# A graph network with two expert stages on one core: blocks hand over their last stores, their semaphores and their first sums

## The reference

```
mean(v) = sum over edges into v of v[src] / max(degree, 1)
x = x + conv2(relu(conv1(norm(x))))     # first graph step; conv(v) = mean(v) @ Wl.T + b + v @ Wr.T
x = x + sum over the 2 chosen of 8 experts: gelu(norm(x) @ W1 + b1) @ W2 + b2
x = x + conv2(relu(conv1(norm(x))))     # second graph step, other weights
x = x + shared MLP + weighted sum over the 2 chosen of 4 small experts
```

## Time and profile before

| what | us |
|---|---|
| median of three runs | 1396.93 (1392.34 to 1399.44) |
| the profiled execution: time | 1399.89 |
| its span, first to last instruction | 1398.4 |
| PE busy in it | 1236.1 (88%) |
| DVE, ACT, POOL busy | 576.2, 400.8, 164.0 |
| borders, by the start of the next block's work | 85.1, 325.4, 828.9, 1030.3, 1247.0 |

### The profile page before, as it was taken

The page is one execution under the profiler, slowest core; times in us unless marked ns, Lnnn a source line. Parts: engine busy times, 40 slices in busy tenths (PEclk is TensorE's granted clock), DMA queues, the critical chain, the costliest instruction groups (busy, mean ns, idle before and its releaser), DMA issues. The chain is left out here.

```text
span 1398.4 us, 22052 instructions
## 1 busy us (share of the span) xinstructions
PE 1236.1 (88%) x7906; PEld 920.5 (66%) x7906; DVE 576.2 (41%) x1495; ACT 400.8 (29%) x798; POOL 164.0 (12%) x177
## 2 busy tenths in 40 slices
PE   5959999998999897299999929999989999979997
PEld 4647778775668674188888827755546677856675
DVE  7857777753436536200000026300024453256443
ACT  3444443431221000164446414300012211123322
POOL 4000000000000424234434410000000000000000
PEclk9979999999999987599999969999999999989999
DMA  6200000015642324435663532120036534125001
GB/s 194 72 22 9 17 17 8 17 42 126 172 134 80 107 72 131 138 61 112 123 137 61 98 80 94 38 82 27 27 92 175 149 121 127 56 87 169 19 19 35
DMA packets 133066, 117.03 MB, mean 84 GB/s; under 512 B 22690, under 2 KB 121379, under 8 KB 132992
## 3 DMA queue, kind: packets, MB, share of 16 engines
q1 hardware_dynamic: 100896, 74.71, 19.0%
q0 software_dynamic: 11984, 18.77, 7.0%
q10 hardware_dynamic: 20112, 22.56, 4.8%
HBM read 67.01 MB, written 48.99 MB: 83 GB/s over the span
## 5 line engine op out<-in xcount | busy, mean ns | idle before, releaser
L1242 PE MATMUL b_pa<-adj,l_parts 128*128 (+1 forms) x1100 | 144.6, 286 | 1.9 <-ACT ring L1164 1.9
L1180 ACT ACTIVATE adj<-b_pw 128x450 f32 (+1 forms) x176 | 87.1, 550 | 137.9 <-PE b_pw L1231 137.9
L1242 PEld LDWEIGHTS b_pa<-adj,l_parts 128*128 128x128 f16 x1100 | 105.6, 98 | 26.2 <-ACT adj L1180 2.0
L543 DVE TENSOR_TENSOR ring<-it,key 128x1800 f16<-128x1800 f16 x88 | 96.2, 1094 | 57.2 <-PE b_pw L1231 55.3
L2246 DVE TENSOR_TENSOR ring<-l_sum,l_parts 128x512 f32<-128x512 f32 x28 | 19.4, 692 | 225.6 <-DMA x<-ring,l_ids_now 140.1
L1231 PE MATMUL b_pw<-ring,room 128*128 128x150 f16 x1056 | 86.3, 233 | 27.7 <-DVE room L543 18.2
L2187 PE MATMUL l_sum<-l_parts,ring 128*128 128x256 f32 x448 | 104.1, 385 | 6.6 <-DVE ring L2246 2.9
L1904 PE MATMUL l_sum<-l_parts,adj 128*128 128x256 f16 x750 | 94.3, 285 | 10.8 <-issue 10.8
L1231 PEld LDWEIGHTS b_pw<-ring,room 128*128 128x128 f16 x1056 | 76.5, 100 | 34.3 <-DVE room L543 21.8
L2187 PEld LDWEIGHTS l_sum<-l_parts,ring 128*128 128x128 f32 x448 | 82.8, 190 | 23.5 <-ACT ring L2232 10.9
L1904 PEld LDWEIGHTS l_sum<-l_parts,adj 128*128 128x128 f16 x750 | 74.9, 102 | 30.2 <-issue 18.9
(11 more groups left out here) (364 smaller groups left out, 1774.2 us busy)
## 6 DMA issues: line engine op xcount, KB each, us to landing
ring<-sums_and_zt SPq DMA_DIRECT2D x50, 256.0 KB, 3.2
l_parts<-in_L_ffn_W SPq DMA_DIRECT2D x16, 512.0 KB
ring<-slots_in SPq DMA_DIRECT2D x28, 257.0 KB
pre<-room ACTq DMA_DIRECT2D x34, 128.0 KB, 1.9
ring<-inv SPq DMA_DIRECT2D x50, 64.0 KB, 3.8
ring<-x SPq DMA_DIRECT2D x5, 640.0 KB, 4.9
sums_and_zt<-room ACTq DMA_DIRECT2D x5, 640.0 KB, 3.1
adj<-xt SPq DMA_DIRECT2D x5, 640.0 KB, 4.5
```

The lines of the kernel that those rows point to most:

```text
L543: return nc.vector.tensor_tensor(out.rearrange("p r (h two) -> p r h two", two=2), names[:, 0:width].rearrange("p (h two) -> p h two", two ...
L1180: ins = nc.scalar.activation(adj[:, :, ds(group * GW * W + b * BANKW * W, BANKW * W)].rearrange("p k (w j) -> p w k j", j=W), pw[u % SLOT ...
L1242: ins = nc.tensor.matmul(pa[f][:, :], parts[:, k, a, f * P:(f + 1) * P], adj[:, k, ds(r * BW, BW)], start=k == 0 and a == 0, stop=k == TIL ...
```

## The change

- **Last stores.** The waits for the last stores at the ends of blocks 1, 2 and 4 go. Their semaphores (`zt_out`, `inverse_out`, `sums_out0`, `sums_out1`) now live through the whole program, and the next block waits where it needs the data: `rows_left` in `build_counts` (POOL before it fills `adj`, ACT before its first counts, SP before the loads ahead), and in `second_conv` SP between the second and the third load of rows. The waits at the ends of blocks 3 and 5 stay.
- **Semaphores.** At a block's end they are only put on a list; POOL clears them in the next block (`clear_used`), so that one drain, one clear and the second barrier go at each border. The program's own end keeps them.
- **No drain.** `Block(no_gpsimd_drain=True)`: POOL doesn't drain at a block's end.
- **First sums.** `neighbours(0)`, `neighbours(1)`, `relu(0)` and `relu(1)` run at the end of blocks 2 and 4, on DVE after its other work (`sum_first`) and on ACT before the last sums (block 2) or before the last but one (block 4; `relu_first`). `second_conv` starts with their semaphores counted up.
- **Last experts.** PE's wait for `ready` moves from its start to the second layer's products.

```diff
-        ctx.callback(self.clear)
-    def clear(self):
-        if self.sems:
+        ctx.callback(self.leave)
+    def leave(self):
+        if self.used is None:
             self.nc.clear_and_free_semaphores(self.sems)
             self.nc.all_engine_barrier(sem_only=True)
+        else:
+            self.used += self.sems
+    def block(self):
+        return self.ctx.enter_context(self.nc.Block(no_gpsimd_drain=True))
+    def clear_used(self):
+        if self.used:
+            self.nc.clear_and_free_semaphores(list(self.used))
+            self.used.clear()
...
 weigh_and_sum
-        block.vector(norm.vector)
+        @block.vector
+        def _(dve):
+            norm.vector(dve)
+            work.sum_first(dve, ahead_in, 16 * (2 + 2 * LOADED), ahead_chain, ahead_summed)
...
-            for u in range(2):
-                sp.wait_ge(sums_out[u], 16 * len(SUM_BLOCKS[u::2]))
...
+                if n == len(SUM_BLOCKS) - 2:
+                    work.relu_first(act, ahead_summed)
...
 first_block
-            sp.wait_ge(zt_out, 16 * len(QUADS))
-            sp.wait_ge(inverse_out, 16)
...
 build_counts
+        def rows_left(eng):
+            eng.wait_ge(g["zt_out"], 16 * len(QUADS))
+            eng.wait_ge(g["inverse_out"], 16)
...
+            rows_left(pool)
             nc.gpsimd.memset(adj[:, :, NWIN:ROWS], 0.0).then_inc(s["ready"], 1)
             nc.gpsimd.memset(ones[:, :], 1.0).then_inc(s["ready"], 1)
+            pr.clear_used()
...
+            work.sum_first(dve, s["ahead_in"], 16 * (2 + 2 * LOADED), s["ahead_chain"], s["ahead_summed"])
...
+                rows_left(act)
                 for u in range(UNROLL):
                     take_counts(0, u)
...
+                work.relu_first(act, s["ahead_summed"])
                 take_sums(BODIES - 1)
...
-            sp.wait_ge(s["sums_out"], 16 * BODIES)
...
 Work
+    def sum_first(self, dve, loaded, count, chain, summed):
+        ch = Chain(dve, chain)
+        dve.wait_ge(loaded, count)
+        for k in range(LOADED):
+            self.add_neighbours(self.nc, ch, k).then_inc(summed, 1)
+    def relu_first(self, act, summed):
+        for k in range(LOADED):
+            act.wait_ge(summed, k + 1)
+            self.relu(self.nc, k)
...
 second_conv
-            for k in range(XB):
+            for k in range(XB - 1):
                 load_x(k)
+            for sem, count in sums_left:
+                sp.wait_ge(g[sem], count)
+            load_x(XB - 1)
...
+            pr.clear_used()
...
-            for k in range(RING - 1):
+            dve.sem_inc(s["h_sum"], LOADED)
+            for k in range(LOADED, RING - 1):
                 neighbours(k)
...
-            for k in range(RING - 1):
+            act.sem_inc(s["h_done"], LOADED)
+            for k in range(LOADED, RING - 1):
                 relu(k)
...
 last_experts
-            pe.wait_ge(s["ready"], 1)
...
                         elif kind == "E2":
+                            pe.wait_ge(s["ready"], 1)
```

More of the change, by code:

```diff
@@ L1319, with __init__ @@
 class Work:
-    def __init__(self, io, g, room, ring):
-        self.io, self.g, self.room, self.ring = io, g, room, ring
+    def __init__(self, nc, io, g, room, ring):
+        self.nc, self.io, self.g, self.room, self.ring = nc, io, g, room, ring
         self.w = room[:, 0:2 * KD * D].rearrange("p (k n) -> p k n", k=KD)
         self.slot = ring[:, 0:RING * 5 * P].rearrange("p (r q) -> p r q", r=RING)
+        self.h, self.zt = (self.slot[:, :, a * KD * P:(a + 1) * KD * P].rearrange("p r (f n) -> p r f n", f=KD) for a in range(2))
+        self.inv = self.slot[:, :, 2 * KD * P:5 * P]
     def selections(self):
@@ L1346, in load_first_rows, with add_neighbours, relu @@
                       rows[0:CH, :].rearrange("(t p) d -> p t d", p=P)).then_inc(self.g["rows_ahead"], 16)
+    def add_neighbours(self, nc, ch, r):
+        h = self.h[:, r, :, :]
+        ch.done(nc.vector.scalar_tensor_tensor(h, h, self.g["unscale"][:, 0:1],
+                                               self.inv[:, r, :].unsqueeze(1).broadcast_to([P, KD, P]), ALU.mult, ALU.mult))
+        return nc.vector.tensor_tensor(h, h, self.zt[:, r, :, :], ALU.add)
+    def relu(self, nc, r):
+        return nc.scalar.activation(self.h[:, r, :, :], self.h[:, r, :, :], ACT.Relu)
+    def sum_first(self, dve, loaded, count, chain, summed):
[7 more added lines that the diff above has]
+            self.relu(self.nc, k)
     def load_sums(self, eng, k, sem):
@@ L1457, in second_conv @@
         split = lambda ap, shape, names: ap.rearrange(f"p ({names}) -> p {names}", **shape)
-        h, zt = (work.slot[:, :, a * KD * P:(a + 1) * KD * P].rearrange("p r (f n) -> p r f n", f=KD) for a in range(2))
-        inv = work.slot[:, :, 2 * KD * P:5 * P]
+        h = work.h
         late = split(ring[:, :], dict(t=2 * CT), "t d")
@@ L1513, in second_conv @@
             + tuple(f"scattered{c}" for c in range(FINISHES))}
-        block = ctx.enter_context(nc.Block())
+        block = pr.block()
         tiles_in = lambda c: slice(STARTS[c], STARTS[c + 1])
@@ L1599, in feed @@
                 with pool.If(flag != 0):
+                    if t == 0:
+                        for sem, stored in sums_left:
+                            pool.wait_ge(g[sem], stored)
                     for n in range(t, t + count):
@@ L1794, in relu @@
                 act.wait_ge(s["h_sum"], k + 1)
-                nc.scalar.activation(h[:, r, :, :], h[:, r, :, :], ACT.Relu).then_inc(s["h_done"], 1)
+                work.relu(nc, r).then_inc(s["h_done"], 1)
             def store_pre(k):
@@ L2561, in program @@
         pr = Prog(nc, ctx)
+        g["used_sems"] = []
+        for name in ("zt_out", "inverse_out", "sums_out0", "sums_out1"):
+            g[name] = pr.sem(name)
         g["ident"] = pr.sb("ident", [P, P], F32)
@@ L2572, in program @@
         parts = held.enter_context(nc.sbuf_tensor("l_parts", [P, TILES, 2, D], F16))
-        work = Work(io, g, room, ring)
+        work = Work(nc, io, g, room, ring)
         with ExitStack() as keys:
@@ L2592, in program @@
         second_conv(nc, io, g, adj, parts, "l1b_", ("L1_gnn_w2_l", "L1_gnn_b2", "L1_gnn_w2_r"),
-                    ("L1_ffn_gW", "L1_ffn_gb"), g["x1"], g["x3"], work, final=final)
+                    ("L1_ffn_gW", "L1_ffn_gb"), g["x1"], g["x3"], work, [(f"sums_out{u}", SUMS_LEFT[u]) for u in range(2)], final=final)
         last_experts(nc, io, g, g["x3"], out, final, parts[:, :, :, :].rearrange("p t a d -> p (t a d)").bitcast(F32), ring)
```

62 lines of the change are left out of this document (33 added, 29 removed).

## The result

The changed kernel takes 1385.04 us (median of 8 runs, 1380.19 to 1392.37) against 1397.62 us for the kernel before beside it (8 runs). The ratio is 0.9925, 95% interval [0.9901, 0.9948]: 0.75% faster, about 10.5 us, or 7 to 14 by the interval. The forecast was 1388.9 us. The profiled execution of the changed kernel took 1383.73 us, its span 1382.3.

The account below looks back on a forecast made before the run. PE, busy in 88% of the span, was taken as the bound, with no engine computing in the border stretches to be cut. 3.1 - 0.5 + 4.2 - 0.55 + 0.75 + 1.0 = 8.0 us off 1396.93 gave 1388.9 us; range 1382.0 to 1394.5.

Parts of the forecast that it names:

- One of the signs that the prediction named for being wrong: At the start of `early(0)`: the prediction is wrong if PE's clock reads 1.00 there.
- the term for the clock: Borders 2 and 4: PE idles right before `early(0)`, which then runs at half clock, losing 2.3 us each.
- Border 1 (+3.1): Start of block 2: the store's wait (2.5 us) and one barrier with its clear (0.6) go, gaining 3.1 us.
- PE's branch stays and moves along: Start of block 2: PE's branch of 3.92 us keeps its length and only starts sooner.
- Borders 2 and 4 (-0.5, -0.55): Starts of `second_conv`: loads gain 1.8 and 1.75 us, the half clock takes 2.3 at each, so a small net loss.
- The rival in which the clock eats nothing: Borders 2, 4 and 5: no half clock loss, so 13.4 us gained in all, 1383.5 us; chance 0.22.
- Border 3 (+4.2): Start of block 4: without POOL's drain DVE begins 3.05 us sooner, ACT in time gives 1.2, gaining 4.2 us.
- That POOL's drain would come back ahead of the clear: Block 4: POOL's 6.8 us drain still comes, before its clear, where nobody waits for it.
- The rival of late rows: Border 3: loads sharing the transfer engines delay chunk 0, gain there 1.4 us, 1391.7 us in all; chance 0.20.
- Border 5 (+0.75): Start of the last stage: one barrier (0.7) and `ready` (0.8) go, half clock takes 0.8 more, net 0.75 us.
- End (+1.0): Program's end: POOL's drain of 0.55 us and one barrier of 0.5 go, gaining 1.0 us.
- Slower by code fetching: All five borders: shorter waits no longer hide instruction fetching, 3.92 us each, 1408.5 us in all; chance 0.06.

Follow-up runs that it names:

- b1: The kernel before with its five Blocks ending without GpSimd's drain, nothing else changed; one time, 1384.9 us.
- b2: The kernel before with its five Blocks ending without GpSimd's drain, the same kernel timed twelve times; ratio 0.9973 to the kernel before.
- u1: The changed kernel with GpSimd's drain back at each Block's end; ratio 0.9942 to the kernel before.
- u3: The changed kernel with the first two tiles' sums and relus back at the start of `second_conv`; ratio 0.9917 to the kernel before.
- u5: The changed kernel with PE's wait for `ready` back at the start of the last stage; ratio 0.9937 to the kernel before.
- u4: The changed kernel with the last stores waited for in their own blocks again; ratio 0.9955 to the kernel before.
- n2: The changed kernel with PE's two branches in `build_counts` exchanged, the path taken here standing first; ratio 0.9895 to the kernel before.
- u2: The changed kernel with semaphores cleared at each block's own end again, with drain and second barrier; ratio 0.9883 to the kernel before.
- v2: v1 with 28 extra products at the start of block 4 on PE, their results overwritten; ratio 0.9914 to the kernel before.
- n1: The changed kernel with DVE's and ACT's first two high and low parts ahead of slots 2 and 3 in `second_conv`; ratio 0.9908 to the kernel before.
- v1: The changed kernel with the edits of n1 and n2 together; ratio 0.9877 to the kernel before.

## Why the prediction held, and where it failed

The time lay in the range and the sign was right. The sum of 8.0 us was too small against some 10.5, and it held terms that were wrong in both directions. The range was 12.5 us wide, so the time lying in it says little for the terms. One of the signs that the prediction named for being wrong came up in the first profile: PEclk was 1.00 when `early(0)` started at border 2. So the term for the clock failed, as a rule, although the time was met.

- **Border 1 (+3.1):** measured +2.49; on the mean of before, b1 and b2 against that of after, u1, u3 and u5 it is 8.70 - 6.28 = 2.4. The step that failed here is "PE's branch stays and moves along": it grew by 0.7 (u4 brings 3.82 us back). The cheapest 4.5 us of the program lay in that row (n2), and I had only carried it over. The upper bound of 3.6 has no row behind it; the store and a barrier of 0.9 make 3.4.
- **Borders 2 and 4 (-0.5, -0.55):** `dense(0)` came 2.95 us sooner after the store, as said (3); the loads gained 1.4 and 1.4 for `early(0)` (1.8 and 1.75 expected). The term of -2.3 for the clock was the largest mistake. It is real, 4.41 us instead of 2.36, but not the rule: over after, u1 to u5 and n2, in 14 such places, `early(0)` ran at half clock in four (after and n2 at border 4, u1 and u5 at border 2). The times from `early(0)` to `dense(2)` were 4.25, 3.80, 3.52 and 4.24 there instead of 2.20, so 7.0 us over 14 places, 0.5 each. The idle stretches in front were 4.66, 2.54, 1.99 and 3.71 us in the four, 1.05 to 3.22 in the ten. On the mean of after, u1, u2, u5 and n2 `dense(2)` comes 12.25 and 13.06 us after the store, in the three with the old waits 13.44 and 13.94: gains of **+1.2 and +0.9**. Behind `early(24)` the same means are 105.41 and 104.49 at border 2, 105.95 and 105.15 at border 4: +0.9 and +0.8. The rival in which the clock eats nothing was nearer than the forecast, but its 1.8 and 1.75 for the loads were too high. The Trainium skill ("TensorE: Matmul & The Clock Gate", "Why this matters for your kernels") has idle gaps put the clock down; by these runs they may or may not. In front of `early(0)` four gaps of fourteen did; behind the wait of about 3 us inside block 5 (v2 above) it was nine of twelve.
- **Border 3 (+4.2):** measured +4.92. The rows landed sooner than taken (4.45 to DVE's start, 5.1 expected). That POOL's drain would come back ahead of the clear was false (u2, b1), at no cost to the sum: nobody waits there. The rival of late rows fell.
- **Border 5 (+0.75):** the barrier with its clear gives 4.07 - 3.34 = 0.73 (b1 and b2 against after), `ready` 0.6 (u5): +1.3. The profile before showed 1.2 more, from an `xt` store that landed late in that execution (4.0 us after its issue, in b1 and b2 2.4; 5.28 us to SP's first load, 4.07 in b1 and b2), which isn't the change's.
- **End (+1.0):** measured +1.03.
- **The first sums ahead (0):** 0 (u3).
- **Slower by code fetching:** no new branch of microseconds stands at a border; border 1 pays 0.7 us for a longer one.

With these sizes the sum is 2.4 + 1.2 + 4.9 + 0.9 + 1.3 + 1.0 = 11.7 us, or 11.3 with the gains behind `early(24)`, inside the measured 7 to 14. The two spans differ by 16.1 us; from the last sums' store of block 2 to the load at border 3 they differ by 498.57 - 492.47 = 6.1, of which 1.4 are border 2. The other 4.7 us aren't shown to be the change's: that stretch took from 477.6 us (b2, without the change) to 502.1 (u4, with most of it), and on one chip 490.4 in b1 and 497.8 in n1. Another 1.7 us of the 16.1 are the half clock inside block 5, which the profile before had (4.46 us) and the one after hadn't (2.79).

## What to carry to other kernels

Read the drains, branches and barriers of the sequencers as rows of their own: here one flag gave 5.7 of 11.7 us by the distances (3.7 as timed, 0.7 to 6.6 by its interval), and the order of two branches, which the change left alone, 4.5. After a load has been taken off the start of a block, go through the lists of the engines behind it again: what stood in a good order for the late operand may now hold up others. But follow the gain until the engine runs without waits again: n1 brought `early(0)` forward by 3 us at each place, and 24 tiles later 0.7 us of it was left at one and nothing at the other. Count a clock penalty by how often it occurs, not by its full size, and don't fill gaps with idle products without seeing the whole span.

## What the runs showed of the hardware

- The Block's drain of POOL at border 3 took 6.845 us behind POOL's indirect transfers (the last two issued at 815.20 and 817.05 in before), to the nanosecond the same in before and u1; a drain in front of a semaphore clear in the same place took at most 0.174 us (u2) and 0.179 (b1).
- PE's branch at the start of block 2, taken over the other path, took 3.76 to 4.80 us, about 0.7 more where the block starts soon after the store's issue. Not taken it took 0.08, and the one that ends the first path and passes over the other took 0.31 (n2, v1) and 0.41 (v2).
- Where in a restart the half clock falls differs between executions of near-identical programs: it reached `early(0)` behind 1.99 us of idleness (u1, border 2), and did not behind 3.22 us (u3, border 4). Inside block 5 a wait of 2.81 to 3.17 us was followed by it in nine kernels of twelve, at 1.7 us each (4.46 against 2.79 for the same 24 products).
